# A pipelined Mamba and mixture-of-experts block on one core: the middle block's two roots on two engines, second products and copies in another order, a re-ordered beginning

## The chip, the cores and the metric

The kernel runs on one core of one Trainium2 chip. The metric is the device time of one execution in microseconds. Four compute engines work beside each other and meet through semaphores: TensorE (PE in the rows, its weight loads PEld), VectorE (DVE), ScalarE (ACT) and GpSimd (POOL); a fifth, SyncE (SP), issues the DMAs.

## The reference, cut to what matters

```python
x = x + 0.5 * ffn(layernorm(x))      # f1: 8 experts, the best one by a gate is taken
x = x + mamba(layernorm(x))          # p: "the middle block"
x = x + 0.5 * ffn(layernorm(x))      # f2: the same experts

def ffn(x):                          # 8192 tokens of 128 values
    idx = argmax(softmax(x @ Wg + bg))
    h = gelu(x @ W1[e] + b1[e]); y = h @ W2[e] + b2[e]      # expert e = idx

def mamba(x):
    xn = x * rsqrt(mean(x * x) + 1e-6) * norm_w
    x_path, z = split(xn @ in_proj.T)
    x_path = silu(causal_conv4(x_path))
    dt, B, C = ...(x_path);  dt = softplus(dt @ dt_proj.T + dt_b)
    h = exp(dt * A) * h + dt * x_path * B;  y = sum(h * C) + D * x_path      # scan over 256 steps, 16 states
    return (y * silu(z)) @ out_proj.T + x
```

x has the shape (32, 256, 128). The middle block needs two inverse roots of the variance of each token: one of (variance + 1e-5) for the layernorm that the residual carries, and one that joins layernorm and RMS norm, of (variance x (1 + 1e-6) + 1e-11).

## The kernel before, in words

The 8192 tokens are cut into 16 chunks of 512 tokens (4 tiles of 128). An iteration i works on several chunks at once: the state scan of chunk i, the expert block f1 of chunk i + 3 (its statistics and norm of i + 4), the middle block's norm and convolution of chunk i + 2, its projections for i + 1, its output and the block f2 of i - 1, and the second products of f2 of i - 2 and i - 3. Iterations 0 to 15 use the plan STEADY; -4 to -1 (FILL) start the pipeline, 16 (DRAIN) ends it.

An iteration has 16 slots. In slot s VectorE does two units of the scan, 2s and 2s + 1 (`state_unit`, L1040): a scan, and for the units that GpSimd doesn't multiply also the product by C. ScalarE makes the factors dA one slot ahead (`make_decay`, L866), in three buffers, so that unit u waits for the end of unit u - 3. GpSimd makes the products by B three slots ahead (L1253), and the products by C of the pairs 1, 2, 4, 5, 9, 10, 12 and 14 (L1263). TensorE sums the states of a pair of slots in every odd slot (`sum_states`, L656), which frees the buffers that GpSimd fills next. All other work has a place in the plan, by slot: "9.5" is the middle of slot 9's second half on that engine. The order on each engine is what the plan writes; the engines then wait for each other by semaphores.

For an expert block TensorE makes the first products of the eight experts (L610, L611) into the bank PH (two of f1, experts 4 and 6, into PY); ScalarE copies each out (L830, L827), four experts are then run through one gelu in place (L852), and the second products (L644) add up in PY, from which VectorE adds the sum to X (`y_f1`, L1109). Gelu needs another table of ScalarE than exp and log; `gelus` (L843) has a table load ahead of the first gelu and another behind the second. Between its two gelus it takes the copies whose place is (slot, 3). The gelus of f2 stand at 10.5.

The middle block's norm: VectorE makes mean and variance (`stats_p`, L1031 to L1037). At 10.5, ahead of the gelus, ScalarE makes both roots as exp(-0.5 log v) in `log_and_roots_p`: two logs and one exp of 128x8. At 11.0 GpSimd makes -mean, waits for the roots, makes the two values of the residual's scaling (`res`) and norms the rows (`normalize_p`, L1241) for TensorE's transposes ("ln_p", slot 12). In the FILL plans, where ScalarE has no such place, GpSimd makes the roots itself by a power of -0.5, of both at once. ScalarE scales the residual at 13.5 (L817).

```python
    w2=[*[(0, e, s, 1, 2) for e, s in experts(5, 6, 6, 7, 7, 8, 8, 8)],      # slots of f1's second products
```

In slot s the second products stand behind the sum of states, where both have a place in it. `gated0` (VectorE, 9.5, L1129) needs the sum of slot 9; `y_f1` (9.5) needs the second products of all eight experts.

In FILL's iteration -3 the first products of chunk 0 go directly through a gelu out of PSUM (L623, L624, L841), each followed by a second product; iteration -2 does this for chunk 1, and has the middle block's norm, first projections and convolution of chunk 0.

Of the kernel before, what the change touches and what calls it, by code (L numbers as in the profile page):

```python
# [299 lines left out]
def macaron_kernel(nc, x, winT, wx, wxT, wdtT, woT, norm_w, conv_w, conv_b, dt_b, a_log, d_param,  # L300
# [3 lines left out]
    with ExitStack() as ctx:  # L304
# [43 lines left out]
        shift = sb("shift", [P, 2, J])  # L348
        var = sb("var", [P, 2, J])
        roots = sb("roots", [P, 2, J])  # L350
        res = sb("res", [P, 2, J])
# [421 lines left out]
        def _(act):  # L773
# [28 lines left out]
            def log_and_roots_p(it, off):  # L802

                k = 2 * act_roots(2, it.i0 + off)
                it.wait(act, moments[2], off, 1, 1)
                it.wait(act, normed[2], off, 1, 0)
                nc.scalar.activation(var[:, 0, :], mv[:, 2, :, 1], ACT.Ln, bias=eps[:, 0:1])
                nc.scalar.activation(var[:, 1, :], mv[:, 2, :, 1], ACT.Ln, bias=eps_p[:, 0:1], scale=1.0 + RMS_EPS) \
                    .then_inc(log_root[2], 1)
                act.wait_ge(log_root[2], k + 1)  # L810
                nc.scalar.activation(roots[:, :, :], var[:, :, :], ACT.Exp, scale=-0.5).then_inc(log_root[2], 1)
# [538 lines left out]
```

## Time and profile before

| what | value |
| --- | --- |
| median of 3 runs | 1206.37 us (1206.27 to 1208.4) |
| the profiled execution's own time | 1208.04 us |
| its span | 1206.1 us |
| TensorE, VectorE, ScalarE, GpSimd busy | 1045.0, 1003.7, 924.9, 1008.1 us |
| mean granted clock of TensorE | 0.937 |

The profile is of one execution. The span goes from its first to its last instruction; 1.9 us of its own time lie outside. Rows give the start and the duration in us; where a row has a bracket, it gives the idle time of the engine ahead of it and what ended it. "x4" means four instructions merged in one row. Durations of neighbours on one engine overlap by some 0.1 us.

### The profile page before, as it was taken

To read this page: it belongs to the slowest core of one execution; us is meant where nothing else is said; L and a number is where in the kernel's file an instruction comes from. 1 tells how busy PE (TensorE), PEld (TensorE's weight loads), DVE (VectorE), ACT (ScalarE), POOL (GpSimd) and SP (SyncE) were. 2 spreads that over 40 slices of the span, in tenths; PEclk is the share of its full clock that TensorE was granted. 3 is DMA by queue.
4 is the path that set the end of the run, shared out by engine and by line. 5 is a ranking of instruction groups with operands and counts; after the bars stand their busy time and mean duration, and the time that the engine had idled before them with its cause. 6 is when DMAs were issued, how large, how long until landed. Compare 5 with 4: busy or idle time off the path is not lost.

```text
span 1206.1 us, 16727 instructions
## 1 busy us (share of the span) xinstructions
PE 1045.0 (87%) x5380; PEld 544.9 (45%) x5380; DVE 1003.7 (83%) x1638; ACT 924.9 (77%) x1440; POOL 1008.1 (84%) x628
## 2 busy tenths in 40 slices
PE   6896959798989999998989999898989997958688
PEld 3452425253535454453534454453544454524246
DVE  2236999998999899898989899899989899999851
ACT  2367687878989797988989797988989787685551
POOL 1129999988999899998999899998999999999920
PEclk9797979898999899998999899998999998988699
DMA  4033434324142424325143424315142423334000
GB/s 104 1 111 146 140 114 143 113 80 168 29 166 98 149 88 159 105 80 185 30 152 111 145 93 140 125 63 189 43 149 98 148 98 138 118 116 140 9 9 18
DMA packets 61751, 130.05 MB, mean 108 GB/s; under 512 B 7552, under 2 KB 28720, under 8 KB 53472
## 3 DMA queue, kind: packets, MB, share of 16 engines
q1 hardware_dynamic: 61664, 128.98, 31.5%
q8 instruction: 43, 0.70, 0.2%
q14 instruction: 44, 0.36, 0.1%
HBM read 106.94 MB, written 22.02 MB: 107 GB/s over the span
## 4 chain that ended last, share of the span: by engine, by line
PE 42%; ACT 17%; POOL 15%; DVE 13%; issue 11%; DMA 1%; SPq 0%; DVEq 0%; POOLq 0%; ACTq 0%
PE PY L644 12%; POOL hb L1253 9%; PE PH L611 9%; PE G L592 6%; DVE dA L1052 5%; ACT hs L852 5%; POOL hb L1263 4%; PE Y L656 4%; DVE hb L1050 3%; ACT dA L882 3%; PE PH L610 3%; ACT hs L830 2%; DVE hb L1056 2%; PE dA L624 2%; PE G L715 1%
## 5 line engine op out<-in xcount | busy, mean ns | idle before, releaser
L1253 POOL TENSOR_TENSOR hb<-dtx_rep,bs 128x1024 f32<-128x1024 f32 x256 | 598.1, 2358 | 17.6 <-PE Y L656 16.1
L882 ACT ACTIVATE dA<-dt_rep,A 128x512 f32<-128x512 f32 x512 | 341.5, 689 | 96.5 <-DVE hb L1056 87.0
L1052 DVE TENSOR_TENSOR_SCAN dA<-dA,hb 128x512 f32<-128x512 f32 x272 | 331.5, 1219 | 8.3 <-DVE oh L1094 3.0
L1050 DVE TENSOR_TENSOR_SCAN hb<-dA,hb 128x512 f32<-128x512 f32 x240 | 279.0, 1206 | 28.2 <-ACT dA L882 28.0
L1263 POOL TENSOR_TENSOR hb<-hb,cs 128x1024 f32<-128x1024 f32 (+1 forms) x128 | 283.1, 2222 | 10.3 <-DVE hb L1050 10.1
L644 PEld LDWEIGHTS PY<-W,hs 128*128 128x128 f32 x2048 | 248.5, 193 | 64.8 <-issue 61.6
L644 PE MATMUL PY<-W,hs 128*128 128x128 f32 x2048 | 260.9, 280 | 0.0
L611 PE MATMUL PH<-xnT,W 128*128 128x512 f32 x396 | 231.8, 668 | 0.0
L1056 DVE TENSOR_TENSOR hb<-dA,cs 128x512 f32<-128x512 f32 x272 | 188.1, 692 | 19.8 <-DVE dA L1052 0.5
L830 ACT COPY hs<-PH 128x512 f32<-128x512 f32 x198 | 115.2, 582 | 95.1 <-PE PH L611 79.5
L656 PE MATMUL Y<-hb,Sel 128*32 128x512 f32 x1024 | 149.7, 655 | 37.3 <-POOL hb L1263 34.8
L610 PE MATMUL PH<-ohT,Lm 24*128 24x512 bf16 x198 | 77.9, 393 | 64.4 <-ACT hs L830 64.4
L852 ACT ACTIVATE hs<-hs 128x2048 f32<-128x2048 f32 x54 | 103.1, 1915 | 0.3
L610 PEld LDWEIGHTS PH<-ohT,Lm 24*128 24x128 bf16 x198 | 18.0, 91 | 157.6 <-ACT hs L830 121.1
L1069 DVE SCALAR_TENSOR_TENSOR xs<-G,Wc,xs 128x506 f32<-128x506 f32 (+2 forms) x96 | 66.7, 737 | 25.7 <-ACT xs L914 23.2
L611 PEld LDWEIGHTS PH<-xnT,W 128*128 128x128 f32 x396 | 60.8, 193 | 46.6 <-issue 46.6
L1279 POOL TENSOR_TENSOR dt<-dt,sp 128x1024 f32<-128x1024 f32 x16 | 37.9, 2367 | 44.8 <-ACT sp L942 44.7
L656 PEld LDWEIGHTS Y<-hb,Sel 128*32 128x32 f32 x1024 | 22.4, 111 | 103.6 <-issue 69.5
L592 PE MATMUL G<-xs,Wxdt 128*128 128x512 f32 x128 | 58.7, 602 | 1.0 <-DVEq L1098 1.0
L789 ACT ACTIVATE xn<-X,shift,rstd 128x128 f32<-128x128 f32 x124 | 50.8, 482 | 5.0 <-POOL shift L1213 5.0
L715 PE MATMUL G<-Wg,xnT 128*128 128x8 f32 x256 | 37.0, 271 | 18.7 <-ACT xnT L778 17.7
L715 PEld LDWEIGHTS G<-Wg,xnT 128*128 128x128 f32 x256 | 34.2, 208 | 37.1 <-ACT xnT L778 37.1
(111 smaller groups left out, 1136.8 us busy)
## 6 DMA issues: line engine op xcount, KB each, us to landing
dtx_rep<-dtx_rows SPq DMA_DIRECT2D x32, 1024.0 KB, 6.4
dt_rep<-dt_rows SPq DMA_DIRECT2D x32, 1024.0 KB, 7.4
bs<-bc_rows SPq DMA_DIRECT2D x64, 256.0 KB, 3.8
cs<-bc_rows SPq DMA_DIRECT2D x64, 256.0 KB, 3.7
dtx_rows<-dtx SPq DMA_DIRECT2D x32, 256.0 KB, 2.5
dt_rows<-dt SPq DMA_DIRECT2D x32, 256.0 KB, 2.6
X<-in_x SPq DMA_DIRECT2D x16, 256.0 KB, 3.1
out<-X SPq DMA_DIRECT2D x16, 256.0 KB, 2.4
```

Source lines behind the costliest of these rows:

```text
L610: nc.tensor.matmul(bank[:, :], Lm[:, e, :], ohT[:, w, (it.i0 + off) % 2, :], start=True, stop=False)
L611: nc.tensor.matmul(bank[:, :], W1[:, e, :], xnT[:, w, :], start=False, stop=True).then_inc(full, 1)
L644: last = nc.tensor.matmul(PY[:, P * j:P * (j + 1)], hs[:, w, e, P * j:P * (j + 1)], W2[:, e, :], start=False, stop=e == E - 1 and j == J - 1)
L656: last = nc.tensor.matmul(Y[D32 * g:D32 * (g + 1), :], Sel[:, :], hb[:, (2 * k + g // 2) % HR, g % 2], start=k == 0, stop=q == NQ - 1)
L830: nc.scalar.copy(hs[:, w, e, :], PH[:, :]).then_inc(ph_free, 1)
L852: nc.scalar.activation(a, a, ACT.Gelu).then_inc(gelu[w], 1)
L882: nc.scalar.activation(dA[u % NA][:, :], dt_rep[:, h, g, :], ACT.Exp, scale=A[:, h, g, q:q + 1]).then_inc(decay, 1)
L1050: nc.vector.tensor_tensor_scan(x_in_hb, a, x_in_hb, 0.0, ALU.mult, ALU.add).then_inc(scan, 1)
L1052: nc.vector.tensor_tensor_scan(a, a, x_in_hb, 0.0, ALU.mult, ALU.add).then_inc(scan, 1)
L1056: nc.vector.tensor_tensor(x_in_hb, a, cs[:, q, :], ALU.mult).then_inc(prod, 1)
L1253: nc.gpsimd.tensor_tensor(hb[:, s % HR], dtx_rep[:, h, 2 * m:2 * m + 2, :], bs[:, q, None, :].broadcast_to([P, 2, CH]), ALU.mult).then_inc ...
L1263: nc.gpsimd.tensor_tensor(h_in_hb, h_in_hb, cs[:, q, None, :].broadcast_to([P, n, CH]), ALU.mult) \
```

## The change

1. The middle block's two roots are split: GpSimd makes the joined one (`rms`) itself in every iteration, by a multiply-add (`var`) and a power of -0.5 over 4 values (`inverse_root_p`, 11.0), and norms the rows from it; ScalarE makes only the layernorm's root, by the common `log_and_root`, at 11.5 instead of 10.5, so behind the gelus. GpSimd makes the residual's scaling from it in a step of its own (`residual_scale`, 12.0).
2. The copy of expert 5 of f1 moves from (11, 0) to (10, 4), a new place behind the second gelu and ahead of the table load that follows it.
3. f1's second products move to slots 5, 6, 7, 7, 8, 8, 9, 9. `y_f1` moves to 10.0 and `stats_p` to 10.5 on VectorE.
4. ScalarE's copy "ln_p" stands ahead of root_f1 in 12.5.
5. Iterations -3 and -2: three second products of chunk 0 move from -3 to the beginning of -2; norm_f1 moves from 11 to 7.5; oh_f1 comes ahead of y_f1; direct products, ln_p, x1 and x0 of -2 move one slot up; ScalarE's res_p moves from 3.5 to 8.5.

```diff
     w1=[*[(0, e, *at, 3) for e, at in experts((8, 0, 8, 0), (9, 0, 9, 0), (10, 0, 10, 0), (10, 2, 10, 3), (10, 3, 10, 3),
-                                              (11, 1, 11, 0), (12, 0, 12, 0), (12, 2, 13, 0))],
+                                              (11, 1, 10, 4), (12, 0, 12, 0), (12, 2, 13, 0))],
...
-    w2=[*[(0, e, s, 1, 2) for e, s in experts(5, 6, 6, 7, 7, 8, 8, 8)],
+    w2=[*[(0, e, s, 1, 2) for e, s in experts(5, 6, 7, 7, 8, 8, 9, 9)],
...
-         "ln_f2": 9.5, "root_p": 10.5, "gelu_f2": 10.5, "ln_p": 12.5,
+         "ln_f2": 9.5, "gelu_f2": 10.5, "root_p": 11.5, "ln_p": 12.5,
...
-         "y_f1": 9.5, "stats_p": 10.0, "gate_f2": 11.0, "stats_f1": 12.0, "oh_f2": 12.0, "tap01": 15.0, "tap2": 15.5},
-    pool={"root_f2": 6.5, "dt": 7.0, "dtx": 7.5, "root_p": 11.0, "norm_p": 11.0, "root_f1": 12.5},
+         "y_f1": 10.0, "stats_p": 10.5, "gate_f2": 11.0, "stats_f1": 12.0, "oh_f2": 12.0, "tap01": 15.0, "tap2": 15.5},
+    pool={"root_f2": 6.5, "dt": 7.0, "dtx": 7.5, "root_p": 11.0, "norm_p": 11.0, "res_p": 12.0, "root_f1": 12.5},
...
     -3: Plan(
...
-        w2=[(0, e, 4 + e, 2, 3) for e in range(E)],
-        act={"ln_f1": 0, "norm_f1": 11}, dve={"gate_f1": 0, "oh_f1": 1, "stats_f1": 2}, pool={"root_f1": 0},
+        w2=[(0, e, 4 + e, 2, 3) for e in range(5)],
+        act={"ln_f1": 0, "norm_f1": 7.5}, dve={"gate_f1": 0, "oh_f1": 1, "stats_f1": 2}, pool={"root_f1": 0},
...
     -2: Plan(
-        stages=[("ln_f1", 0, 0), ("gate_f1", 0, 1), ("oh_f1", 1, 0), ("ln_p", 6, 0), ("x1", 7, 0), ("x0", 7, 1)],
-        direct=[(0, e, *at, 3) for e, at in experts((2, 1, 2), (3, 1, 3), (4, 1, 4), (5, 1, 5), (6, 1, 7), (8, 1, 8),
-                                                    (9, 1, 9), (10, 1, 10))],
-        act={"ln_f1": 0, "res_p": 3.5, "ln_p": 6, "taps": 7.5, "norm_f1": 8.5},
-        dve={"gate_f1": 0, "y_f1": 1, "stats_p": 1.5, "oh_f1": 2, "stats_f1": 3, "tap01": 8, "tap2": 8.5},
-        pool={"root_p": 1, "norm_p": 1.5, "root_f1": 5}, sp={"x_in": 0}),
+        stages=[("ln_f1", 0, 0), ("gate_f1", 0, 1), ("oh_f1", 1, 0), ("ln_p", 5, 0), ("x1", 6, 0), ("x0", 6, 1)],
+        direct=[(0, e, *at, 3) for e, at in experts((1, 1, 1), (2, 1, 2), (3, 1, 3), (4, 1, 4), (5, 1, 5), (6, 1, 7),
+                                                    (8, 1, 8), (9, 1, 9))],
+        w2=[(0, 5, 0, 0, 2), (0, 6, 0, 1, 2), (0, 7, 0, 1, 2)],
+        act={"ln_f1": 0, "ln_p": 5, "taps": 6.5, "res_p": 8.5, "norm_f1": 8.5},
+        dve={"gate_f1": 0, "oh_f1": 0.25, "y_f1": 0.5, "stats_p": 1, "stats_f1": 3, "tap01": 8, "tap2": 8.5},
+        pool={"root_p": 1, "norm_p": 1.5, "res_p": 4, "root_f1": 5}, sp={"x_in": 0}),
...
-            def log_and_roots_p(it, off):
...
             def scale_residual(it, off):
 
                 it.wait(act, xr_ready, off, 1, 1)
+                it.wait(act, rooted[2], off, 1, 1)
...
                         nc.scalar.activation(a, a, ACT.Gelu).then_inc(gelu[w], 1)
+                    take_units(it, s, 3 + k)
                     if k == 0:
-                        take_units(it, s, 3)
...
-            def inverse_roots_p(it, off):
+            def inverse_root_p(it, off):
...
+                nc.gpsimd.tensor_scalar(var[:, :], mv[:, 2, :, 1], 1.0 + RMS_EPS, RMS_EPS * LN_EPS, ALU.mult, ALU.add) \
+                    .then_inc(pool_ln[2], 1)
+                pool.wait_ge(pool_ln[2], n + 2)
+                nc.gpsimd.tensor_tensor(rms[:, :], var[:, :], half[:, :], ALU.pow).then_inc(pool_ln[2], 1)
+
+            def residual_scale(it, off):
+
+                n = roots_before(2, it.i0 + off) + 3
                 if root_on_act(2, it.i0 + off):
                     pool.wait_ge(log_root[2], 2 * act_roots(2, it.i0 + off) + 2)
+                else:
+                    nc.gpsimd.tensor_tensor(vt[:, 2, :], mv[:, 2, :, 1], eps[:, :], ALU.add).then_inc(pool_ln[2], 1)
                     pool.wait_ge(pool_ln[2], n + 1)
...
+                    nc.gpsimd.tensor_tensor(rstd[:, 2, :], vt[:, 2, :], half[:, :], ALU.pow).then_inc(pool_ln[2], 1)
+                    pool.wait_ge(pool_ln[2], n + 2)
+                nc.gpsimd.tensor_scalar(res[:, :], rstd[:, 2, :], 1.0, 1.0, ALU.mult, ALU.add)
+                nc.gpsimd.tensor_tensor(shift[:, 2, :], neg[:, 2, :], rstd[:, 2, :], ALU.mult).then_inc(rooted[2], 1)
 
             def normalize_p(it, off):
 
-                it.wait(pool, rooted[2], off, 1, 1)
+                pool.wait_ge(pool_ln[2], roots_before(2, it.i0 + off) + 3)
```

Iteration -1 gets `"res_p": 7.5` on GpSimd. One memset of VectorE at the start goes with `eps_p`.

## Rows read from the trace of the kernel before

**Rows 1.** The page's first part: busy us, share of the span, instructions.
```profile
PE 1045.0 (87%) x5380; PEld 544.9 (45%) x5380; DVE 1003.7 (83%) x1638; ACT 924.9 (77%) x1440; POOL 1008.1 (84%) x628
```

**Rows 2.** Timeline of VectorE, "out" of three iterations: start, duration, operation.
```profile
448.64 0.69 DVE L1109 SCALAR_TENSOR_TENSOR X<-Y,X 128x512 f32<-128x512 f32 x1
...
516.54 0.69 DVE L1109 SCALAR_TENSOR_TENSOR X<-Y,X 128x512 f32<-128x512 f32 x1
...
585.22 0.69 DVE L1109 SCALAR_TENSOR_TENSOR X<-Y,X 128x512 f32<-128x512 f32 x1
```

**Rows 3.** Windows: width, busy PE, PEld, DVE, ACT, POOL, clock, DMA share, GB/s.
```profile
143.00:206.00 63.00, 47.09 (x240) 23.14 (x240) 59.30 (x94) 48.59 (x79) 62.38 (x39) 0.86 0.36 125
...
516.50:585.20 68.70, 63.85 (x337) 33.63 (x336) 62.27 (x101) 59.01 (x93) 62.66 (x39) 0.95 0.34 117
...
550.00:556.30 6.30, 6.27 (x14) 2.41 (x14) 4.40 (x14) 5.84 (x8) 5.04 (x4) 0.50 0.15 52
```

**Rows 4.** The chain of waits in order of time, one period.
```profile
473.04 0.69 DVE X L1109
...
475.10 1.13 DVE dA L1052
```

**Rows 5.** Timeline of ScalarE in slots 10 to 12.
```profile
477.05 0.69 ACT L882 ACTIVATE dA<-dt_rep,A 128x512 f32<-128x512 f32 x1 [2.04 <-DVE hb L1056]
477.68 0.28 ACT L807 ACTIVATE var<-mv,eps 128x4 f32<-128x4 f32 x1
...
478.40 1.28 ACT L852 ACT_TABLE_LOAD   x1
...
485.69 0.59 ACT L830 COPY hs<-PH 128x512 f32<-128x512 f32 x1
...
489.12 0.29 ACT L798 ACTIVATE vt<-mv,eps 128x4 f32<-128x4 f32 x1
```

**Rows 6.** Timeline of TensorE, slots 8 and 11.
```profile
466.72 2.84 PE L644 MATMUL PY<-W,hs 128*128 128x128 f32 x24
...
482.14 0.39 PE L610 MATMUL PH<-ohT,Lm 24*128 24x512 bf16 x1 [2.36 <-ACT hs L830]
```

**Rows 7.** Timeline of VectorE, its waits in slots 9 to 12.
```profile
472.43 0.69 DVE L1129 TENSOR_TENSOR y<-Y,zs 128x512 f32<-128x512 f32 x1 [0.71 <-PE Y L656]
...
484.01 0.41 DVE L1105 COPY ohT<-G 24x512 bf16<-24x512 bf16 x1 [0.46 <-PE G L724]
...
486.90 2.34 DVE L1050 TENSOR_TENSOR_SCAN hb<-dA,hb 128x512 f32<-128x512 f32 x2 [1.23 <-ACT dA L882]
```

**Rows 8.** Timeline of GpSimd, the block's "neg" and three waits of a round.
```profile
478.54 0.19 POOL L1220 TENSOR_SCALAR neg<-mv 128x4 f32<-128x4 f32 x1
...
489.72 0.20 POOL L1213 TENSOR_TENSOR shift<-neg,rstd 128x4 f32<-128x4 f32 x1 [2.60 <-ACT rstd L800]
...
518.97 4.66 POOL L1253 TENSOR_TENSOR hb<-dtx_rep,bs 128x1024 f32<-128x1024 f32 x2 [1.22 <-PE Y L656]
...
530.04 2.37 POOL L1279 TENSOR_TENSOR dt<-dt,sp 128x1024 f32<-128x1024 f32 x1 [1.26 <-ACT sp L942]
```

**Rows 9.** Timeline of GpSimd, its first product and its first long wait at the end.
```profile
94.02 18.49 POOL L1253 TENSOR_TENSOR hb<-dtx_rep,bs 128x1024 f32<-128x1024 f32 x8 [1.48 <-DMA dtx_rep<-dtx_rows]
...
1150.44 2.35 POOL L1263 TENSOR_TENSOR hb<-hb,cs 128x1024 f32<-128x1024 f32 x1 [4.08 <-DVE hb L1050]
```

**Rows 10.** Groups by line: count, busy us, mean ns, idle ahead; GpSimd's powers.
```profile
L1211 POOL TENSOR_TENSOR rstd<-vt,half 128x4 f32<-128x4 f32 x5 | 5.1, 1014 | 0.4
...
L1230 POOL TENSOR_TENSOR roots<-var,half 128x8 f32<-128x8 f32 x2 | 3.3, 1647 | 0.2
```

**Rows 11.** GpSimd's products by B: shortest, median, longest ns; first and last start.
```profile
L1253 POOL TENSOR_TENSOR hb<-dtx_rep,bs x256: 2339/2357/2388, 94.0 to 1144.0; 128x1024 f32<-128x1024 f32 x128
```

**Rows 12.** Timeline of TensorE and ScalarE in the fill.
```profile
45.58 0.60 PE L623 MATMUL PH<-ohT,Lm 24*128 24x512 bf16 x1 [1.99 <-DVE ohT L1105]
...
65.36 0.59 ACT L959 COPY Wxdt<-Y 128x512 f32<-128x512 f32 x1 [0.21 <-PE Y L663]
```

More of the change, by code:

```diff
@@ L141 @@
         dve={"gate_f1": 2, "oh_f1": 4, "y_f1": 5, "stats_p": 5.5, "stats_f1": 6, "tap01": 12, "tap2": 12.5},
-        pool={"dt": 4, "dtx": 4.5, "root_p": 6.5, "norm_p": 7, "root_f1": 9},
+        pool={"dt": 4, "dtx": 4.5, "root_p": 6.5, "norm_p": 7, "res_p": 7.5, "root_f1": 9},
         sp={"x_in": 0, "bc": 2, "b0": 3, "b1": 3, "c0": 3, "b2": 4, "c1": 4, "b3": 5, "c2": 5, "c3": 5, "dt": 6, "dtx1": 7,
@@ L225, in roots_before @@
 def roots_before(w, chunk):
-    return sum(1 if root_on_act(w, c) else 4 if w == 2 else 3 for c in range(chunk))
+    return sum((2 if w == 2 else 0) + (1 if root_on_act(w, c) else 3) for c in range(chunk))
 def on_pool(s):
@@ L339, in macaron_kernel @@
         eps = sb("eps", [P, J])
-        eps_p = sb("eps_p", [P, 1])
-        half = sb("half", [P, 2, J])
+        half = sb("half", [P, J])
         stat = sb("stat", [P, 3, J, 6])
@@ L347, in macaron_kernel @@
         rstd = sb("rstd", [P, 3, J])
[L348 to L351, printed above, removed]
+        shift = sb("shift", [P, 3, J])
+        var = sb("var", [P, J])
+        rms = sb("rms", [P, J])
+        res = sb("res", [P, J])
         xn = sb("xn", [P, 2, J, H])
@@ L463, in macaron_kernel @@
                 *[(Wo[:, h, :], wo_rows[h]) for h in range(HF)]]
-        N_ZERO = 4
+        N_ZERO = 3
         N_MASK = 6
@@ L744, in body @@
                         pe.wait_ge(w2_in, 16)
-                    if (it.i0, s) == (-2, 7):
+                    if (it.i0, s) == (-2, 6):
                         pe.wait_ge(set_up, N_SET)
@@ L800, in log_and_root @@
                 nc.scalar.activation(rstd[:, w, :], vt[:, w, :], ACT.Exp, scale=-0.5).then_inc(log_root[w], 1)
-            def log_and_roots_p(it, off):
[L804 to L811, printed above, removed]
             def scale_residual(it, off):
                 it.wait(act, xr_ready, off, 1, 1)
+                it.wait(act, rooted[2], off, 1, 1)
                 for j in range(J):
                     last = nc.scalar.activation(rows(it, off, j), rows(it, off, j), ACT.Identity,
-                                                scale=res[:, 0, j:j + 1], bias=res[:, 1, j:j + 1])
+                                                scale=res[:, j:j + 1], bias=shift[:, 2, j:j + 1])
                 last.then_inc(normed[2], 1)
@@ L894, in stages @@
                         copy_out(it, f"ln_f{w + 1}", xnT[:, w, :])
+                if t == at.get("ln_p") and it.has(2):
+                    copy_out(it, "ln_p", xrT[:, :])
                 if t == at.get("root_f2") and it.has(-1):
@@ L899, in stages @@
                 if t == at.get("root_p") and it.has(2):
-                    log_and_roots_p(it, 2)
+                    log_and_root(it, 2, 2)
                 if t == at.get("norm_f2") and it.has(-1):
                     normalize(it, 1, -1)
-                if t == at.get("ln_p") and it.has(2):
-                    copy_out(it, "ln_p", xrT[:, :])
                 if t == at.get("res_p") and it.has(2):
@@ L954, in body @@
                 for s in range(SLOTS):
-                    if (it.i0, s) == (-2, 7):
+                    if (it.i0, s) == (-2, 6):
                         act.wait_ge(rest_in, 16 * len(rest))
@@ L1220, in inverse_roots_p @@
                 nc.gpsimd.tensor_scalar(neg[:, 2, :], mv[:, 2, :, 0], -1.0, 0.0, ALU.mult, ALU.add).then_inc(pool_ln[2], 1)
+                nc.gpsimd.tensor_scalar(var[:, :], mv[:, 2, :, 1], 1.0 + RMS_EPS, RMS_EPS * LN_EPS, ALU.mult, ALU.add) \
[4 more added lines that the diff above has]
+                n = roots_before(2, it.i0 + off) + 3
                 if root_on_act(2, it.i0 + off):
                     pool.wait_ge(log_root[2], 2 * act_roots(2, it.i0 + off) + 2)
+                else:
+                    nc.gpsimd.tensor_tensor(vt[:, 2, :], mv[:, 2, :, 1], eps[:, :], ALU.add).then_inc(pool_ln[2], 1)
                     pool.wait_ge(pool_ln[2], n + 1)
-                else:
-                    nc.gpsimd.tensor_scalar(var[:, 0], mv[:, 2, :, 1], 1.0, LN_EPS, ALU.mult, ALU.add) \
-                        .then_inc(pool_ln[2], 1)
-                    nc.gpsimd.tensor_scalar(var[:, 1], mv[:, 2, :, 1], 1.0 + RMS_EPS, RMS_EPS * LN_EPS, ALU.mult, ALU.add) \
-                        .then_inc(pool_ln[2], 1)
-                    pool.wait_ge(pool_ln[2], n + 3)
-                    nc.gpsimd.tensor_tensor(roots[:, :, :], var[:, :, :], half[:, :, :], ALU.pow).then_inc(pool_ln[2], 1)
-                    pool.wait_ge(pool_ln[2], n + 4)
-                nc.gpsimd.tensor_scalar(res[:, 0], roots[:, 0], 1.0, 1.0, ALU.mult, ALU.add)
-                nc.gpsimd.tensor_tensor(res[:, 1], neg[:, 2, :], roots[:, 0], ALU.mult).then_inc(rooted[2], 1)
+                    nc.gpsimd.tensor_tensor(rstd[:, 2, :], vt[:, 2, :], half[:, :], ALU.pow).then_inc(pool_ln[2], 1)
+                    pool.wait_ge(pool_ln[2], n + 2)
+                nc.gpsimd.tensor_scalar(res[:, :], rstd[:, 2, :], 1.0, 1.0, ALU.mult, ALU.add)
+                nc.gpsimd.tensor_tensor(shift[:, 2, :], neg[:, 2, :], rstd[:, 2, :], ALU.mult).then_inc(rooted[2], 1)
             def normalize_p(it, off):
-                it.wait(pool, rooted[2], off, 1, 1)
+                pool.wait_ge(pool_ln[2], roots_before(2, it.i0 + off) + 3)
                 if it.has(off - 1):
@@ L1241, in normalize_p @@
                     last = nc.gpsimd.tensor_scalar(xr[:, j:j + 1, :], X[:, it.tiles(off, j, 1), :], neg[:, 2, j:j + 1],
-                                                   roots[:, 1, j:j + 1], ALU.add, ALU.mult)
+                                                   rms[:, j:j + 1], ALU.add, ALU.mult)
                 last.then_inc(xr_ready, 1)
@@ L1271, in stages @@
                 if t == at.get("root_p") and it.has(2):
-                    inverse_roots_p(it, 2)
+                    inverse_root_p(it, 2)
                 if t == at.get("norm_p") and it.has(2):
                     normalize_p(it, 2)
+                if t == at.get("res_p") and it.has(2):
+                    residual_scale(it, 2)
                 if t == at.get("root_f1") and it.has(4):
```

5 lines of the change are left out of this document (2 added, 3 removed).

## The prediction

> **What bounds the kernel now.** I read the busy shares first [rows 1]: TensorE 87%, GpSimd 84%, VectorE 83%, ScalarE 77%. No engine is full, so waits set the time. The distance between two "out" additions of VectorE gives the period of an iteration [rows 2]: 67.90 and 68.68 us, which alternate through the middle, mean 68.3. The longer kind has a granted clock of 0.95, owing to a window of 6.3 us at 0.50 [rows 3].
>
> Then the chain of waits inside one period [rows 4]. In slots 4 to 9 it is TensorE (24 second-product matmuls up to 469.6 [rows 6]), then the sum of states, then VectorE: y_f1, the block's statistics, unit 20. The product of unit 20 frees the buffer that ScalarE's unit 23 needs (477.05), and only behind it come the two roots, the table load and the gelus [rows 5]. TensorE stands still for 2.36 us meanwhile, as PH is emptied only behind the first gelu [rows 6]. Behind the second table load ScalarE goes on without a pause from expert 5's copy through slots 11 to 14, which carries the delay to VectorE: its waits here are 0.71 us before gated0, 0.46 before oh_f2 and 1.23 before unit 24 [rows 7]. GpSimd waits 2.60 + 1.22 + 1.26 us [rows 8] and 0.15 for its own "neg", so its own round is 67.9 - 5.2 = 62.7. VectorE's, with the waits of rows 7 taken off, is 67.9 - 2.4 = 65.5, and less by what it waits elsewhere.
>
> Only the middle goes so. In the first round GpSimd is busy for 62.38 of 63 us [rows 3] and sets the time; and in the last three rounds it does so again, up to 1146.4, where it first waits long, 4.08 us [rows 9].
>
> **The change, part by part, in one steady period.**
>
> *Second products.* Before, 24 matmuls (three experts) stand directly ahead of the sum of slot 9; after, experts 6 and 7 come behind it. Two experts are 16 of those 24, some 1.9 us, so the sum ends at 470.5 instead of 472.4. VectorE arrives at 469.39 + 2.33 = 471.7, so its 0.71 us wait ends, and gated0 ends at 472.35. y_f1 must still wait for expert 7, whose work now ends where the sum ended, 472.4. So y_f1 starts at about 472.45, not 473.04: **-0.6**. Cover: experts 2 to 5 need only gelus made long before, and the freed PH waits fall in ScalarE's idle time. The tight place is the sum of slot 7, now 0.95 us earlier (about 460.65) while GpSimd's products 4 and 5 end at 460.4; if GpSimd is late there, each us is lost.
>
> *Statistics.* They move behind units 20 and 21, and VectorE was busy there anyway; unit 20, at 475.10 before, can follow y_f1 (473.04 and 0.69 long) directly [rows 4]: **-1.26**. VectorE's total is the same. GpSimd reads the moments at 478.54 [rows 8] and they are ready at about 477.5: hidden, with 1 us of cover.
>
> *Roots.* Two logs and an exp in front of the gelus take 477.68 to 478.40, 0.72 us [rows 5]; they leave. One log and one exp come at slot 11.5, still inside ScalarE's unbroken stretch: the same pair in root_f1 takes 0.43. Net **-0.29**. The ln_p copy passes root_f1 by 0.43 us, ahead of which TensorE has finished; root_f1's result had GpSimd waiting 2.60 us, which the next item uses up.
>
> *GpSimd.* It gains "var" (0.28 until the next begins) and a 4-element power, 1.01 us in the fill where GpSimd makes it, plus 0.1 of gap [rows 10]; and loses 0.15 of wait. I take +1.35 us per iteration. No row has a power beside a full VectorE; the ends are 1.01 and the 8-element 1.65 [rows 10], so 1.35 to 2.0. norm_p ends near 482.05, not 481.09; TensorE, then at e6, reaches the transposes near 482.9: hidden, 0.8 of cover. At slot 12.0 GpSimd waits for ScalarE's root: ScalarE has it at 483.5 + 1.24 + 0.43 = 485.2, GpSimd arrives at 485.6: nothing, 0.4 of cover. Behind it stand bx 15 and the shift of f1; then GpSimd is 1.0 us ahead of before where the others are 2.15 ahead, and its waits of 1.22 and 1.26 take the difference. Its round becomes 62.7 + 1.35 = 64.1 (64.8 at the upper price), below the 65.75 which I expect for the period.
>
> The GPSIMD Engine Reference of the Trainium skill (Key points) says that GpSimd shares its SBUF interfaces with VectorE and meets contention from instructions with two SBUF inputs. The 256 products by B last 2339 to 2388 ns from the idle fill to the full middle [rows 11], so the sum leaves it out; by the rule the power might be held longer, which is a rival below.
>
> *Expert 5's copy ahead of the table load.* ScalarE does the same work in another order: 0. TensorE's expert 7 gets PH earlier, which is slack. ScalarE's block from unit 23 to the end of the second load was 8.63 us (477.05 to 485.69 [rows 5]); it becomes 8.63 - 0.72 + 0.48 = 8.4, so the load ends at 475.1 + 8.4 = 483.5, 2.15 us earlier; the stretch behind it loses the copy's 0.48 and gains the root's 0.43.
>
> Sum: 0.6 + 1.26 + 0.29 = **2.15 us per iteration**. VectorE has 0.71 + 0.46 + 1.23 = 2.4 of wait to give, so it can follow.
>
> *The clock.* In the longer period TensorE stands at 0.50 (1.2 GHz) from 550.0 to 556.3 [rows 3], right after the round's long idling, the place of 482.14 one round earlier [rows 6]; this makes 0.78 us of period [rows 2], in five of the rounds. The wait of 2.36 us nearly ends: expert 5 can follow the sum at 479.8. If every such drop ends with the idling, that is 3.9 us, if each only moves, 0; I take 1.6. The Trainium skill (TensorE: Matmul & The Clock Gate, What's actually happening) sets the clock by how busy TensorE has recently been; the idling ahead of this drop agrees, and by it the whole 3.9 would come.
>
> *Beginning.* The xn of chunk 1 is made in a pause of ScalarE two gelus earlier, at 32.8 instead of 37.2, and e5 to e7 of chunk 0 move behind the transposes. Transposes start at 36.7, gate at 38.2, one-hot ends at 40.8, its transposes follow e7 at 41.1, and the copy oh_f1 now comes ahead of y_f1 and the statistics: TensorE's direct products start at 42.0, not 45.58 [rows 12]: -3.5. But the residual's scaling (1.64 us), which filled an idle gap at 51.3, now stands before xn at 8.5, behind the gelu of e6 (whose product ended at 63.1 and now at 59.6): 59.6 + 0.6 + 1.6 + 1.6 + 0.6 gives the Wxdt copy at 64.0, not 65.36 [rows 12]: -1.35. GpSimd's first bx keeps its distance to this (its extra vt and power, 0.4 net, lie in the 1.48 us wait for dtx_rep [rows 9]): **-1.5** (ends -1.35 and -2.0, the latter by TensorE's 0.6 us wait for xr).
>
> **The sum over the kernel.** Beginning -1.5. Round 0 to 1, on GpSimd: +1.3. Round 1 to 2: -2.1. Ten rounds in the middle: -21.5. Clock: -1.6. Round 12 to 13, which takes 65.8 and then can't fall below 64.2: -1.6. The root of iteration 13 lies on GpSimd's last unbroken stretch: +1.3. The end is not changed. In all -25.7: 1208.04 of the profiled execution becomes 1182.3. The profiled one is 1.7 us over the median of 1206.37, so the median becomes **1180.7, say 1181**.
>
> **The rivals.**
>
> *A, GpSimd becomes the bound of the middle.* For: 1.6 us of room is all it has, and its waits come for different partners, so they need not all vanish: with one of the two (1.22 or 1.26) and the upper price of the power left the round is 66.0, with both 67.3. Against: its waits [rows 8] are for partners which move earlier. At 66.7 each round gains 0.95 less: -25.7 + 11 x 0.95 = -15: 1191.
>
> *B, the clock gives it all.* No drop in the middle and fewer at the start, where round 0 has 0.86 [rows 3]: some 4 us more: 1176.
>
> *C, slower.* The power on GpSimd is held up by VectorE's traffic. GpSimd's round is above the old 68.3 if the power takes over 1.01 + (68.3 - 64.1) = 5.2 us; at 6.5 us the period is 69.6 and the kernel 12 x 1.3 + 2 x 5.5 longer, 1233. Against: the small operations in the busy middle take 0.19 and 0.20, as in the fill.
>
> *D, it doesn't do what it says:* something else holds unit 23 or the gelus at 477 to 480, and only the fill is left, minus GpSimd's ends: 1206 - 1.5 + 2.6 = 1207. ScalarE's own order has nothing else there.
>
> **How the numbers follow.** My forecast 0.60, A 0.17, B 0.12, C 0.05, D 0.06. The likeliest one's own range is 1177 to 1186 (price of the power, 0 or 3.9 us of clock, beginning by 0.6). B and A inside gives 1173 to 1194, with C and D outside. A measurement tells 0.2%, 2.4 us, from no change. Faster: 0.60 + 0.17 + 0.12 and a sliver of D: 0.90; same 0.04; slower 0.06.
>
> **What the profile after would show.** VectorE's "out" additions 65.5 to 66 us apart; no wait before gated0; ScalarE's dA of unit 23 1.9 us earlier in the round, followed at once by the gelu's table load; TensorE's PH wait of 2.36 gone; VectorE without waits at oh_f2 and unit 24; GpSimd's waits down to some 1.5 us per round. GpSimd's "neg" to first xr shows the power: 1.5 us. TensorE's first direct product of chunk 1 at 42. Wrong it would be if sum_states in slots 7 or 11 waits for GpSimd, if GpSimd waits at slot 12, or if the clock falls inside slots 4 to 9, where TensorE's time is the period's.

## The result and the profile after

The changed kernel takes 1177.42 us (median of 4 runs, 1173.58 to 1179.07) against 1206.32 (median of 4, 1205.49 to 1208.4). The ratio is 0.9753, 95% interval 0.9725 to 0.9782: 2.5% faster. The forecast was 1181, range 1173 to 1194. The profiled execution took 1179.07 us with a span of 1177.3, 28.8 less than before.

The page's first part answers to [rows 1]:

```profile
PE 1033.7 (88%) x5380; PEld 546.0 (46%) x5380; DVE 1000.8 (85%) x1637; ACT 919.1 (78%) x1426; POOL 1024.5 (87%) x658
```

GpSimd is busy 16.4 us longer in a shorter span, the others less. VectorE's "out" additions, from the timeline, answer to [rows 2]:

```profile
504.77 0.69 DVE L1098 SCALAR_TENSOR_TENSOR X<-Y,X 128x512 f32<-128x512 f32 x1
570.29 0.69 DVE L1098 SCALAR_TENSOR_TENSOR X<-Y,X 128x512 f32<-128x512 f32 x1
635.82 0.69 DVE L1098 SCALAR_TENSOR_TENSOR X<-Y,X 128x512 f32<-128x512 f32 x1
702.23 0.69 DVE L1098 SCALAR_TENSOR_TENSOR X<-Y,X 128x512 f32<-128x512 f32 x1
```

The period is 65.52 us, twice 66.4 in the middle, where before it was 67.9 and 68.7 by turns. The windows of a short and of a long round (columns as in [rows 3]) show that the long one has a lower clock, and that GpSimd is busy for 63.49 of 65.5 us:

```profile
504.80:570.30 65.50, 61.04 (x337) 32.80 (x336) 61.97 (x102) 58.44 (x92) 63.49 (x41) 1.00 0.36 122
635.80:702.20 66.40, 62.44 (x337) 33.52 (x336) 61.99 (x101) 58.67 (x92) 64.38 (x42) 0.97 0.36 120
```

The timelines of one period, which begins with the "out" of 504.77. VectorE, for [rows 4] and [rows 7]: y_f1, unit 20, and the pair that begins with unit 24:

```profile
528.73 0.69 DVE L1098 SCALAR_TENSOR_TENSOR X<-PY,X 128x512 f32<-128x512 f32 x1 [0.30 <-PE PY L644]
529.34 1.22 DVE L1041 TENSOR_TENSOR_SCAN dA<-dA,hb 128x512 f32<-128x512 f32 x1
...
540.61 2.31 DVE L1039 TENSOR_TENSOR_SCAN hb<-dA,hb 128x512 f32<-128x512 f32 x2
```

ScalarE, for [rows 5]: the two table loads, expert 5's copy between gelu and load, and the block's log behind them:

```profile
532.10 1.28 ACT L842 ACT_TABLE_LOAD   x1
...
537.96 0.59 ACT L820 COPY hs<-PH 128x512 f32<-128x512 f32 x1
538.57 1.28 ACT L848 ACT_TABLE_LOAD   x1
...
541.10 0.28 ACT L798 ACTIVATE vt<-mv,eps 128x4 f32<-128x4 f32 x1
```

TensorE, for [rows 6]: PH is free when the sum ends. The sum of slot 11 waits 0.37 us for GpSimd (0.23 before, at 478.71). And behind it stands a pause of 1.41 us that was 0.32 before (at 488.09):

```profile
534.84 1.06 PE L656 MATMUL Y<-hb,Sel 128*32 128x512 f32 x8 [0.37 <-POOL hb L1256]
535.84 0.38 PE L610 MATMUL PH<-ohT,Lm 24*128 24x512 bf16 x1
...
542.20 0.38 PE L641 MATMUL PY<-b_part,ohT 24*128 24x128 bf16 x4 [1.41 <-issue]
```

GpSimd, for [rows 8]: its one wait of the round, and "neg" to the norming with the power between:

```profile
518.28 2.36 POOL L1274 TENSOR_TENSOR dt<-dt,sp 128x1024 f32<-128x1024 f32 x1 [1.27 <-ACT sp L932]
...
534.66 0.19 POOL L1209 TENSOR_SCALAR neg<-mv 128x4 f32<-128x4 f32 x1
534.93 0.20 POOL L1210 TENSOR_SCALAR var<-mv 128x4 f32<-128x4 f32 x1
535.21 1.02 POOL L1213 TENSOR_TENSOR rms<-var,half 128x4 f32<-128x4 f32 x1
536.35 1.74 POOL L1234 TENSOR_SCALAR xr<-X,neg,rms 128x128 f32<-128x128 f32 x4
```

And the beginning, for [rows 12], TensorE's first two direct products of chunk 1 and ScalarE's Wxdt copy:

```profile
40.89 0.38 PE L623 MATMUL PH<-ohT,Lm 24*128 24x512 bf16 x1 [0.51 <-DVE ohT L1094]
...
42.27 0.38 PE L623 MATMUL dA<-ohT,Lm 24*128 24x512 bf16 x1
...
57.27 0.57 ACT L949 COPY Wxdt<-Y 128x512 f32<-128x512 f32 x1
```

**Where the time went**, told at GpSimd's "neg" of the block, whose starts lie at 137.54, 202.23, 271.31, 928.71 and 993.25 us, and before at 143.34, 206.21, 273.13, 956.11 and 1022.96:

| stretch | predicted | measured |
| --- | --- | --- |
| beginning, to the first "neg" of a steady round | -1.5 | -5.8 |
| round 0 to 1 | +1.3 | +1.8 |
| round 1 to 2 | -2.1 | +2.2 |
| ten middle rounds, their clock in it | -23.1 | -25.6 |
| round 12 to 13 | -1.6 | -2.3 |
| from there to the end | +1.3 | +0.9 |
| sum | -25.7 | -28.8 |

The middle is near the forecast. Two terms at the start are off by 4.3 us each, with opposite signs. The experiments therefore ask three things: what each part of the change is worth in the middle, whether GpSimd (47% of the chain of waits after, 15% before) has become the bound, and what made the start.

### The profile page after: what moved, and what is told of

The parts are those of the page before. It is cut to its first block, busy times and chain, and to the rows that moved or that the text cites. A ratio compares the mean times of both kernels' runs of the same rounds, so it can differ in the third digit from the quotient of the medians.

```text
span 1177.3 us, 16745 instructions
## 1 busy us (share of the span) xinstructions
PE 1033.7 (88%) x5380; PEld 546.0 (46%) x5380; DVE 1000.8 (85%) x1637; ACT 919.1 (78%) x1426; POOL 1024.5 (87%) x658
## 4 chain that ended last, share of the span: by engine, by line
POOL 47%; PE 23%; issue 19%; ACT 5%; DVE 5%; DMA 0%; POOLq 0%; DVEq 0%; ACTq 0%
POOL hb L1246 25%; POOL hb L1256 15%; PE PY L644 6%; PE PH L611 4%; PE Y L656 3%; POOL dt L1274 3%; POOL dtx L1279 3%; PE G L592 2%; PE dA L624 2%; DVE dA L1041 2%; PE PH L610 1%; DVE hb L1039 1%; PE PY L611 1%; ACT hs L842 1%; ACT dA L872 1%
## 5 line engine op out<-in xcount | busy, mean ns | idle before, releaser
L644 PEld LDWEIGHTS PY<-W,hs 128*128 128x128 f32 x2048 | 251.9, 195 | 76.1 <-issue 72.8
L644 PE MATMUL PY<-W,hs 128*128 128x128 f32 x2048 | 267.6, 282 | 0.0
L611 PE MATMUL PH<-xnT,W 128*128 128x512 f32 x396 | 227.3, 656 | 0.0
L656 PE MATMUL Y<-hb,Sel 128*32 128x512 f32 x1024 | 152.2, 666 | 48.8 <-POOL hb L1256 42.5
L592 PE MATMUL G<-xs,Wxdt 128*128 128x512 f32 x128 | 62.3, 632 | 1.0 <-DVEq L1087 1.0
```

What stands on the lines that cost most here:

```text
L611: nc.tensor.matmul(bank[:, :], W1[:, e, :], xnT[:, w, :], start=False, stop=True).then_inc(full, 1)
L644: last = nc.tensor.matmul(PY[:, P * j:P * (j + 1)], hs[:, w, e, P * j:P * (j + 1)], W2[:, e, :], start=False, stop=e == E - 1 and j == J - 1)
L656: last = nc.tensor.matmul(Y[D32 * g:D32 * (g + 1), :], Sel[:, :], hb[:, (2 * k + g // 2) % HR, g % 2], start=k == 0, stop=q == NQ - 1)
```

## The experiments

Times are medians; the kernel before was run beside each, with medians from 1205.8 to 1206.2. "Period" is the distance of two "out" additions at full clock, read from each profile. The changed kernel itself was run a second time, with the last three:

> The changed kernel once more, unchanged, as the measure for the others on the same chip and for how much its beginning and its end vary between executions: 1177, period 65.52, first bx between 83 and 88 us.

Measured: 1177.73 us, ratio 0.9761 (0.974 to 0.9782), period 65.52, first product by B on GpSimd at 87.71. Over the eight profiles of kernels with the new beginning and split roots (seven kernels, whose beginning is written alike) this product starts anywhere from 83.2 to 87.8, and the period of the changed kernel is the same in its two profiles. Small effects are therefore read from the period.

Most of that spread arises ahead of the part that was re-ordered. At first TensorE needs 2.08 us for the two matmuls of 128x512 of a direct product, later 1.12, and the moment at which this changes lies just ahead of 20 us in one profile and behind 26 us in another, with the same order of work in both (the clock column of the windows gives 1.00 there in both). So the eighth direct product of chunk 0, the last piece of the beginning that no edit moved, starts anywhere from 31.7 to 35.7 us over the fourteen profiles. Its start in the kernel before, in the changed kernel and in the one below that keeps TensorE busy:

```profile
35.27 0.38 PE L623 MATMUL dA<-ohT,Lm 24*128 24x512 bf16 x1
...
34.52 0.38 PE L623 MATMUL dA<-ohT,Lm 24*128 24x512 bf16 x1
...
33.06 0.38 PE L623 MATMUL dA<-ohT,Lm 24*128 24x512 bf16 x1
```

Distances from this start to the first "neg" of a steady round are free of that part of the spread, and are used below.

**The parts in the middle.** Second products back:

```diff
-    w2=[*[(0, e, s, 1, 2) for e, s in experts(5, 6, 7, 7, 8, 8, 9, 9)],
+    w2=[*[(0, e, s, 1, 2) for e, s in experts(5, 6, 6, 7, 7, 8, 8, 8)],
```

> The changed kernel with the second products of f1 back in slots 5, 6, 6, 7, 7, 8, 8, 8. Theory: 16 more matmuls ahead of the sum of slot 9, VectorE waits 0.7 us before gated0 and y_f1 starts 0.6 us later: 12 x 0.6 = +7: 1184, period 66.1. Rival (GpSimd sets the period): 0 to +2.

Measured: 1181.69, ratio 0.9816 (0.978 to 0.9851); period 65.94, so +0.42 (predicted 0.6), between the two expectations and nearer to the theory. Statistics back:

```diff
-         "y_f1": 10.0, "stats_p": 10.5, "gate_f2": 11.0, "stats_f1": 12.0, "oh_f2": 12.0, "tap01": 15.0, "tap2": 15.5},
+         "y_f1": 10.0, "stats_p": 10.0, "gate_f2": 11.0, "stats_f1": 12.0, "oh_f2": 12.0, "tap01": 15.0, "tap2": 15.5},
```

> The changed kernel with the block's statistics back at 10.0, ahead of units 20 and 21. Theory: unit 20 ends 1.26 us later, unit 23 and the gelus too, 12 x 1.26 = +15: 1192, period 66.8. Rival (GpSimd sets the period and the other chain has room): the period rises by 1.26 less that room, below 66.2: under 1186.

Measured: 1193.39, ratio 0.9898 (0.9864 to 0.9933); period 66.88, +1.36 (predicted 1.26), as the theory wants. Expert 5's copy back:

```diff
-                                              (11, 1, 10, 4), (12, 0, 12, 0), (12, 2, 13, 0))],
+                                              (11, 1, 11, 0), (12, 0, 12, 0), (12, 2, 13, 0))],
```

> The changed kernel with expert 5's copy back at (11, 0), behind the second table load. Theory: the same work of ScalarE in another order, 0: 1177, period 65.5. Rival (the copy frees PH for expert 7, which TensorE needs early): TensorE waits for PH behind the gelus and the period rises by up to the load's 1.28 us less TensorE's room: up to 1185.

Measured: 1175.66, ratio 0.9768 (0.9731 to 0.9804); period 65.51: nothing, as predicted. Then the roots as before (`log_and_roots_p`, `inverse_roots_p` and the places `"root_p": 10.5` on ScalarE and 11.0 on GpSimd):

```diff
-         "ln_f2": 9.5, "gelu_f2": 10.5, "root_p": 11.5, "ln_p": 12.5,
+         "ln_f2": 9.5, "root_p": 10.5, "gelu_f2": 10.5, "ln_p": 12.5,
...
-    pool={"root_f2": 6.5, "dt": 7.0, "dtx": 7.5, "root_p": 11.0, "norm_p": 11.0, "res_p": 12.0, "root_f1": 12.5},
+    pool={"root_f2": 6.5, "dt": 7.0, "dtx": 7.5, "root_p": 11.0, "norm_p": 11.0, "root_f1": 12.5},
```

> The changed kernel with the roots as before: both on ScalarE at 10.5 ahead of the gelus, none on GpSimd in the steady rounds. Theory (ScalarE, TensorE and VectorE together set the period, GpSimd has room): 0.72 - 0.43 = 0.29 us more per round ahead of the gelus, 12 x 0.29 = +3.5, less 1.3 in round 0 to 1 and 1.3 at the end, where GpSimd loses its power: about 1178 against 1177.4. Rival (GpSimd sets the period now, as the chain of waits says): its round gets 1.35 us shorter and the period falls by up to 1 us until VectorE with its own 64 us holds it: about 1165.

Measured: 1203.56, ratio 0.9986 (0.9968 to 1.0005); period 67.86, **+2.34**. Both expectations failed: this edit alone takes back nearly the whole gain. ScalarE's timeline shows why:

```profile
470.25 0.30 ACT L808 ACTIVATE var<-mv,eps 128x4 f32<-128x4 f32 x1 [1.67 <-DVE mv L1038]
470.45 0.28 ACT L809 ACTIVATE var<-mv,eps_p 128x4 f32<-128x4 f32 x1
470.77 0.21 ACT L812 ACTIVATE roots<-var 128x8 f32<-128x8 f32 x1
471.00 1.28 ACT L853 ACT_TABLE_LOAD   x1
```

The logs wait 1.67 us for the moments, which with late statistics come only now, and the table load stands behind them. It starts 29.73 us behind "out", in the changed kernel 27.33, so 2.40 later: the wait of 1.67 and the 0.75 from the first log to the load. The late statistics are free only when nothing ahead of the gelus reads them. The fourth corner of this square was run to see it from the other side, both edits undone:

> The kernel of x1_roots_joint with the block's statistics back at 10.0, too: both roots on ScalarE ahead of the gelus, statistics ahead of unit 20. Theory (the joint roots wait for late statistics, so the two edits only work together): the roots find their moments, the period is that of before less 0.44 for the second products, 67.5, which is 0.4 shorter than with late statistics, 67.86: 1199. Rival (each edit has its own price, as predicted): 67.86 + 1.26 = 69.1: 1218.

Measured: 1203.03, ratio 0.9977 (0.9962 to 0.9991); period at full clock 67.46, as the theory has it, but most of its rounds take 68.4, with drops of the clock. The logs wait no more, ScalarE's pause stands one instruction earlier, for the product of unit 20:

```profile
470.42 0.69 ACT L883 ACTIVATE dA<-dt_rep,A 128x512 f32<-128x512 f32 x1 [1.42 <-DVE hb L1057]
471.04 0.28 ACT L808 ACTIVATE var<-mv,eps 128x4 f32<-128x4 f32 x1
```

| period at full clock | statistics at 10.0 | at 10.5 |
| --- | --- | --- |
| both roots ahead of the gelus | 67.46 | 67.86 |
| roots split, ScalarE's behind them | 66.88 | 65.52 |

The statistics' move costs 0.40 us with joint roots and gains 1.36 with split ones. The split gains 0.58 or 2.34. Together it is 1.94.

**Is GpSimd the bound now?** The changed kernel's chain, by engine, says nearly so:

```profile
POOL 47%; PE 23%; issue 19%; ACT 5%; DVE 5%; DMA 0%; POOLq 0%; DVEq 0%; ACTq 0%
```

One kernel loads GpSimd more, another takes away its wait. The first:

```diff
+                for k in range(2 if root_on_act(2, it.i0 + off) else 0):
+                    nc.gpsimd.tensor_tensor(spare[:, k, :], var[:, :], half[:, :], ALU.pow)
                 nc.gpsimd.tensor_scalar(res[:, :], rstd[:, 2, :], 1.0, 1.0, ALU.mult, ALU.add)
```

> The changed kernel with two more powers of 128x4 on GpSimd in each steady round at slot 12 (their results are read by nobody), 2.2 us. Theory (GpSimd is busy 64.2 of 65.5 and has only its wait of 1.26 for softplus left): the wait takes 1.26 of it, period 66.5, and the first and the last round lose 2.2 each: 1177.4 + 11 x 0.95 + 4.4 = 1192. Rival A (GpSimd sets the period already, its wait is part of the chain): +2.2 per round, period 67.7: 1206. Rival (more room than its wait): period 65.6: 1182.

Measured: 1195.83, ratio 0.9917 (0.9896 to 0.9937); period 67.27, +1.75, between the theory (66.5) and rival A (67.7).

```profile
546.63 1.98 POOL L1227 TENSOR_TENSOR spare<-var,half 128x4 f32<-128x4 f32 x2 [0.90 <-ACT rstd L801]
548.60 0.20 POOL L1228 TENSOR_SCALAR res<-rstd 128x4 f32<-128x4 f32 x1
```

The powers take 1.97 us, and 0.22 of it is hidden. The wait for softplus does vanish, as the theory wanted, but GpSimd waits 0.90 at ScalarE's root in its place. From that root it then works without a wait to the next "neg", where it waits 0.22 for the moments. On that way the sum of slot 7 waits 1.30 us for GpSimd's product and y_f1 waits 1.26 for TensorE, and ScalarE comes to the next root later by as much: a loop over four engines, read from these waits. (The chain of waits over this stretch shows GpSimd, TensorE and VectorE, and not ScalarE, so the last link is argued.) Work added to GpSimd at this place has 0.2 us of room, not the 1.26 of its wait. Then the softplus addition half a slot later:

```diff
-    pool={"root_f2": 6.5, "dt": 7.0, "dtx": 7.5, "root_p": 11.0, "norm_p": 11.0, "res_p": 12.0, "root_f1": 12.5},
+    pool={"root_f2": 6.5, "dt": 7.5, "dtx": 7.5, "root_p": 11.0, "norm_p": 11.0, "res_p": 12.0, "root_f1": 12.5},
```

> The changed kernel with GpSimd's dt addition at 7.5 instead of 7.0: behind that slot's product by B, directly ahead of dtx, so that GpSimd works through the 1.26 us in which it waits for softplus. If GpSimd's chain with this wait sets the period: up to 1.26 less per round, 11 x 1.26 = 14: 1164. If VectorE, ScalarE and TensorE set it and GpSimd's wait only fills up: period 65.5, 1177, and the wait reappears elsewhere.

Measured: 1174.92, ratio 0.9754 (0.9732 to 0.9776), against 0.9761 for the changed kernel; period 65.52. GpSimd's timeline:

```profile
511.85 2.36 POOL L1274 TENSOR_TENSOR dt<-dt,sp 128x1024 f32<-128x1024 f32 x1
...
526.37 0.20 POOL L1209 TENSOR_SCALAR neg<-mv 128x4 f32<-128x4 f32 x1 [0.30 <-DVE mv L1026]
...
534.27 0.19 POOL L1225 TENSOR_SCALAR res<-rstd 128x4 f32<-128x4 f32 x1 [0.91 <-ACT rstd L800]
```

The wait for softplus is gone and comes back as 0.30 and 0.91, as the second expectation has it: GpSimd does not set the period alone. With the room of 0.2 us this says that two loops tie in the changed kernel, of which its chain shows one (GpSimd has 47% and 49% of the chain in its two profiles, 17% here). In this kernel's chain over the same stretch GpSimd has no piece: it is TensorE without a pause in slots 4 to 9, unit 20 of VectorE, ScalarE's load and gelu, TensorE again with its pause of 1.42 us, and ScalarE's norm of f1.

The last of this group tries for TensorE's 1.41 us:

```diff
-                                              (11, 1, 10, 4), (12, 0, 12, 0), (12, 2, 13, 0))],
+                                              (11, 1, 10, 4), (12, 0, 11, 1), (12, 2, 13, 0))],
...
-    pool={"root_f2": 6.5, "dt": 7.0, "dtx": 7.5, "root_p": 11.0, "norm_p": 11.0, "res_p": 12.0, "root_f1": 12.5},
+    pool={"root_f2": 6.5, "dt": 7.5, "dtx": 7.5, "root_p": 11.0, "norm_p": 11.0, "res_p": 12.5, "root_f1": 12.5},
```

> The changed kernel with GpSimd's dt addition at 7.5, and ScalarE's copy of expert 6 out of PY moved from (12, 0) to (11, 1), between two factors dA and ahead of the block's root; GpSimd's residual scaling at 12.5. Theory (TensorE sets slots 11 to 14, where it stands 1.41 us until that copy has emptied PY): the copy comes 1.08 us earlier, TensorE follows, period 65.5 - 0.4 to 0.9, the kernel 1165 to 1170. Rival (the factor dA that now comes 0.48 us later holds VectorE, or another engine is bound there): period 65.5 or more, 1175 or more.

Measured: 1171.73 (1171.4 to 1173.76), ratio 0.9716 (0.9697 to 0.9735), against 0.9761 (0.974 to 0.9782) for the changed kernel on the same chip: 5.4 us less, by the two intervals 2 to 9. This is the fastest kernel of the study, but not for the reason given: the pause shrinks from 1.41 to 0.39 and the period stays 65.52. ScalarE does the same work in its unbroken stretch, which in this kernel's chain has nearly every piece from the gelus' load to the norm of f1. What is gone are the long rounds: the eight distances from 302 to 826 us are all 65.51 or 65.52, while the second profile of the changed kernel has 66.45 and 66.42 among them. With the dt addition at 7.5 alone two of the eight are 66.43 and 66.46, so they go with the copy. Its two first rounds, "neg" to "neg", take 131.1 together, not 132.9; this comes with the dt addition, which alone has 131.1 too.

```profile
534.94 0.38 PE L641 MATMUL PY<-b_part,ohT 24*128 24x128 bf16 x4 [0.39 <-issue]
```

**The beginning.** The changed kernel with the old iterations -3 and -2 (GpSimd's residual scaling at 2):

```diff
-        w2=[(0, e, 4 + e, 2, 3) for e in range(5)],
-        act={"ln_f1": 0, "norm_f1": 7.5}, dve={"gate_f1": 0, "oh_f1": 1, "stats_f1": 2}, pool={"root_f1": 0},
+        w2=[(0, e, 4 + e, 2, 3) for e in range(E)],
+        act={"ln_f1": 0, "norm_f1": 11}, dve={"gate_f1": 0, "oh_f1": 1, "stats_f1": 2}, pool={"root_f1": 0},
...
-        pool={"root_p": 1, "norm_p": 1.5, "res_p": 4, "root_f1": 5}, sp={"x_in": 0}),
+        pool={"root_p": 1, "norm_p": 1.5, "res_p": 2, "root_f1": 5}, sp={"x_in": 0}),
```

> The changed kernel with the beginning (iterations -3 and -2) as before. Theory from the trace of after (the new beginning keeps TensorE at full clock through the direct products): GpSimd's first bx comes 6 to 8 us later, as before at 94.0, and all of it stays in the time: 1183 to 1185. Rival (the prediction's own term, 1.5 us): 1179.

Measured: 1184.56 (1184.06 to 1185.22), ratio 0.9828 (0.9809 to 0.9847); first product by B at 91.89. Against 0.9761 that is 8.1 us, by the two intervals 4.7 to 11.5. And the other way round, the same lines put into the kernel before (`-` and `+` exchanged, without GpSimd's "res_p", which it doesn't have):

> The kernel before with the new beginning alone (iterations -3 and -2). Theory (what x5_fill_old lost, 7 us, is gained here too): 1199. Rival (in a kernel with the old middle the earlier start is given back, as for x7_busy_fill): 1205.

Measured: 1200.30, ratio 0.9959 (0.9943 to 0.9976), by this ratio 4.9 us less than before (2.9 to 6.9). By both the new beginning is worth more than the predicted 1.5. The traces agree: from the eighth direct product to the first steady "neg" the two profiles with the old beginning take 108.1 and 108.5 us, the eleven with the new one 100.3 to 103.5. To part the clock from the order, the kernel before got matmuls without a purpose in TensorE's pauses of 1.65 and 1.99 us ahead of the direct products:

```diff
+            def keep_busy(n):
+                nc.tensor.matmul(Y[:, :], W1[:, 0, :], W1[:, 0:4, :].rearrange("p e m -> p (e m)"), start=True, stop=True)
+                for _ in range(n):
+                    nc.tensor.matmul(Y[:, :], Lm[:, 0, :], Lm[:, 0:4, :].rearrange("p e m -> p (e m)"), start=True, stop=True)
...
+                    if (it.i0, s) == (-2, 1):
+                        keep_busy(1)
+                    if (it.i0, s) == (-2, 2):
+                        keep_busy(2)
```

> The kernel before with five matmuls more on TensorE in its two pauses ahead of chunk 1's direct products (their results are read by nobody). Nothing else is moved. Theory (the clock makes most of the beginning's gain): the four direct products from 45.6 on come 1.37 us apart instead of 2.54, ScalarE's Wxdt copy at 60.7 instead of 65.4, the kernel 4.7 us shorter: 1201.6. Rival (the order makes it): 1206.

Measured: 1205.27 (10 runs, 1202.05 to 1211.81), ratio 1.0 (0.9982 to 1.0018). Windows of 44 to 56 us, first of this kernel, then of the kernel before:

```profile
44.00:56.00 12.00, 11.53 (x29) 3.60 (x27) 4.62 (x16) 7.70 (x16) 5.33 (x11) 1.00 0.00 0
```

```profile
44.00:56.00 12.00, 10.42 (x14) 3.02 (x15) 4.06 (x24) 3.42 (x8) 5.98 (x14) 0.51 0.00 1
```

The mechanism is there: the clock stays at 1.00 where it was 0.51 (1.2 GHz), twice the matmuls fit in, the products follow each other in 1.37 us instead of 2.54, Wxdt's copy is at 58.18 (before 65.36) and GpSimd's first product at 88.47 (94.02). Of these 5.5 us 2.2 stand ahead of the inserted matmuls (33.06 against 35.27), so 3.3 are theirs. But the time is the same: no gain beyond 2.2 us fits the interval. In the profile 5.3 us, 3.1 without that head start, are still there at the first "neg" and 4.7 (2.5) at the last (1018.28 against 1022.96); the last two "out" additions then lie 60.49 apart instead of 58.06, with the clock at 0.73 from 1150 to 1160 us where the kernel before has 0.99. Such an end of 60.3 to 60.5 stands in five of the fourteen profiles, of kernels with five different middles. Whether an earlier start brings it about, or chance, is left open. So the clock's part of the new beginning is shown up to GpSimd's first product, and not in the kernel's time.

## Why the prediction was right, step by step

- **The bound and the parts.** The steps hold in their order: second products 0.42 (predicted 0.6), roots and statistics together 1.94 (1.55), expert 5's copy 0.0 (0), sum 2.38 (2.15). The waits named vanish: gated0, oh_f2, unit 24, TensorE's 2.36. Behind "out", y_f1 starts 0.44 earlier (predicted 0.6), unit 20 1.89 (1.86) and the gelus' load 2.43. The prices of the single steps were wrong as prices of edits: "statistics -1.26" holds only behind "roots", which then are worth 2.34, not 0.29. The sum did not see that late statistics meet the reader that stands ahead of the gelus, so that the two terms can't be earned one by one.
- **GpSimd.** The power is 1.02 us in the busy middle, the lower end of the 1.01 to 1.65 that bounded it; 1.14 with its gap, and "neg" to the first xr takes 1.69 us instead of 0.81. At slot 12 it arrives just behind ScalarE's root (541.71 behind 541.42 + 0.21), with under 0.1 us of cover instead of 0.4. One of the forecast's own signs of being wrong did come: the sum of slot 11 waits for GpSimd, 0.37 us; but it did so before by 0.23, and the period fell all the same. Rival A's number did not come, but its ground was nearer than its chance said: own round 64.2 under a period of 65.5 looks like 1.3 us of room, and the run with two powers shows 0.2. Rival C is refuted by the same rows: 1.02 here, and 1.98 for two, beside a VectorE whose only pause there is 0.21 us; the contention of which the GPSIMD Engine Reference of the Trainium skill (Key points) speaks is not to be seen in these rows.
- **The clock.** Of the 3.9 us of the long rounds 1.8 come in the changed kernel (4.0 extra before over ten rounds, 2.2 after), predicted 1.6. The changed kernel's pause of 1.41 us stands in every round of the middle; in the long round shown the clock is at 0.50 right behind it, from 674 to 677.6 us, in the short round shown it stays at 1.00. With the copy of expert 6 moved, too, the pause is 0.39 and all of the 3.9 comes. The rule of the Trainium skill (TensorE: Matmul & The Clock Gate, What's actually happening), that recent activity sets the clock, agrees in kind with this, and with the matmuls without a purpose; the whole 3.9, which the prediction took from it for the end of the 2.36 us wait, did not come, as another pause took that wait's place.
- **The beginning** is the term that was mis-sized most: -1.5 predicted, -5.8 in the trace, of which 0.75 stand ahead of the change (34.52 against 35.27), so -5.1; from all profiles the new beginning gives 4.6 to 8.1. The step that failed is the one which let the direct products keep their distance of 2.54 us: that was a duration at half clock, owed to the two pauses ahead of them, and the same edit shortens the pauses to 0.51. At 1.37 us four steps save 4.7 more. The start of the direct products moved by 4.7 (3.5 predicted; 3.9 without the 0.75), and the residual's scaling takes back 1.9 at Wxdt's copy, as said (TensorE ends ahead of it at 55.4, the copy starts at 57.27, behind scaling and xn). Part of the rest is given back in iteration -1, so that 8.1 us at Wxdt's copy are 6.2 at GpSimd's first product. That this shorter way also shortens the kernel is shown for the new beginning as a whole (4.9 and 8.1 us) and not for the clock by itself, whose own run gained nothing.
- **Round 1 to 2** was to gain the middle's 2.1 and lost 2.2. The step that failed is to have put the middle's chain there. In the kernel before and in four others this round takes 65.6 to 67.3, whatever stands at slots 10 and 11; in the seven profiles with split roots and dt at 7.0 it takes 67.0 (three) or 69.1 (four). Where it takes 69.1 TensorE is on the path at half clock:

```profile
216.99 0.60 PE L610 MATMUL PH<-ohT,Lm 24*128 24x512 bf16 x1 [2.53 <-ACT hs L820]
217.52 2.08 PE L611 MATMUL PH<-xnT,W 128*128 128x512 f32 x2
...
229.78 1.58 PE L715 MATMUL G<-Wg,xnT 128*128 128x8 f32 x8 [2.51 <-ACT xnT L778]
```

With the first two rounds taken together, split roots need 132.9 to 133.9 us and joint ones 128.5 to 130.1. In the profile of the changed kernel GpSimd is busy for 63.39 of the 64.69 us of round 0 to 1 and so the bound there. In its second profile that round takes 65.90, GpSimd waits 1.85 us for VectorE's moments at its end, and the next round takes 67.04 with a clock of 0.95 instead of 0.90. Twice the power with "var", 1.4 us a round, would be 2.8 of the 3.1 to 4.1 us that the two rounds lose against the kernel before, but in that profile GpSimd had room; with its wait for softplus worked through they take 131.1. So the cause stays open in part; it was read from traces, the clock among it, and not tried by itself.

The term for round 12 to 13 starts from a round of 65.8, which is the distance of ScalarE's residual scalings; from "neg" to "neg" it was 66.85. The floor of 64.2 was right (64.54 measured), so this term gave 2.3, not 1.6.

The total was nearer than its terms, as two misses of 4.3 us cancelled, which was luck; the middle, 25.6 of the 28.8 us, was right for the reasons given.
